# A two-layer vision tower on one core: tables shifted by products, column sums on VectorE, zeros in pieces, and a new order of the work

## The chip, the cores and the metric

One Trainium2 chip, one of its cores. The time is the device time of one execution in microseconds. Five engines run their own lists of instructions: PE (TensorE), DVE (VectorE), ACT (ScalarE), POOL (GpSimd) and SP, which only issues DMAs. Sixteen DMA engines serve all of them.

## What is computed

```python
h = tok(x, cls_token, cls_pos, ln1, W, bias, ln2)       # (32, 37, 256)
h = concatenate([cls_tok, h], axis=1)                   # (32, 38, 256)
h = h + attn0(layernorm(h))      # 16 heads, causal; weights rounded to -2..2 times their mean |w|
h = h + tanh(layernorm(h) @ W1 @ W2 @ W3 + b)
h = h + attn1(layernorm(h))      # 16 heads, with biases and a mask of heads
h = h + moe(layernorm(h))        # 16 experts of 256-1024-256, top 1, capacity ceil(1216 / 16)

def tok(img, ...):
    x = patches(img)                                    # 6 x 6 patches of 16 x 16 x 3 = 768
    x = layernorm(x) * ln1_g + ln1_b
    x = layernorm(x @ W + bias) * ln2_g + ln2_b
    return concatenate([cls_token + cls_pos, x + sincos_positions], axis=1)
```

Inputs, weights and result are fp32. 32 images of 38 tokens make 1216 rows, held as ten tiles of 128 rows (the last two have 116 and 76). As 38 doesn't divide 128, each tile starts at another phase of the image.

## The kernel before

**Token stage.** The image comes twice: by feature (`in_xf`, the left operand of the product, tile `xT`) and by token (`in_xt`, for the statistics), in five groups of tiles each, `XGROUPS` (L62). The first layernorm is folded into the weights: `tokWg` = `g1` * `tokW` minus a row of column sums. The column sums `cs` (L851 to L858) are six PE products of `gs` with the six blocks of `tokW`; DVE makes `tokWg` from them in six operations (L1259). The bias sums `bs` (L863) are six further products with `be1`. A token tile (`tok`, L897) is six products. DVE then scales it (L1300), takes its statistics (L1245, L1246), and in `tokn` normalises it (L1313) and adds the table of positions at the tile's phase (L1314). POOL forms the inverse roots (L768, L776).

**Tables.** POOL adds up one table `added` (L759). SP copies it with 16 DMAs into `attn1` at the phases of tiles 1 to 8 (`tables`, L521; L672 to L675). The real content of `attn1`, layer 1's weights, is loaded once DVE has the statistics of tile 8 (`a1`, L690 to L692). DVE's `wo` (L1289 to L1292) and PE's `bo` (L888) need it.

**Loads at the start.** SP and ACT issue them in a fixed order (L663 to L680, L1099 to L1109). SP's last four, two groups of `in_xf`, `in_ffn0` and all of `k_empty`, which presets the experts' buffer `expert_in` in HBM, stand behind the table copies. ACT sums the magnitudes of `attn0` (`asum`, L1126). DVE quantises it in `qs`, in six operations over long pieces (L1278 to L1282). PE folds the three matrices of the tanh block in `fB` and `fW` (L881).

**Attention.** Images go in pairs, 16 per layer. Per pair: POOL masks the keys by head (`km`, L791), PE makes the scores (`s`, L945, L950), DVE takes off their maxima (L1321, L1324), ACT the exponentials (L1164), PE transposes them (`pt`, L958) and multiplies with V (`pv`, L969), DVE divides (L1330, L1331), PE transposes again (`ot`, L975). V comes from L932; nine small DMAs per three images spread it over partitions (SP, L708), and POOL masks it (`vb`, L801). Q and K are made for 256 tokens at a time (`qk`, L921), the output projection per tile (`proj`, L983).

**Routing and experts.** Per tile: gate product (`log`, L990), DVE adds the bias, finds the largest value and its index and makes a one-hot row (L1352 to L1358), ACT sums the exponentials (L1182), PE counts (`cnt`, L998 to L1001), DVE makes the slot (L1363 to L1374), POOL scatters the token's row (`scat`, L824). Then twelve passes of expert work (L1024, L1035, L1057) with weights that SP streams in, and an indirect store per pass (L832). Ahead of them PE runs 58 records of filler (L1063).

**Order.** Each engine's order is fixed before the launch by `plan()`. It takes costs (`COST`), handover times (`HANDOVER`), arrival times of loads (`ARRIVES`, `XARRIVES`), and what each step needs (`needs()`). At each step it gives an engine the task with the least start time times `EAGER` plus due time (`wanted()`, from `GOAL`). Three PSUM buffers `G` go round among PE's steps in the order of `tasks`. An engine never leaves this order: where its next step has to wait, all behind it wait.

## Time and profile before

| | us |
|---|---|
| timed runs, median (lowest to highest of 3) | 361.92 (360.45 to 362.28) |
| the profiled execution | 361.07 |
| its span | 359.3 |
| PE busy | 325.1 |
| DVE busy | 195.7 |
| POOL busy | 168.6 |
| ACT busy | 167.7 |

The span runs from the first instruction to the last. Busy time leaves out register and DMA-issuing instructions; matmuls are pipelined and their ends are modelled, so a stretch in which PE is shown busy need not be at its peak. A group's row gives its busy time, the mean of one instruction, and the idle time of the engine before it with what ended that. A matmul in fp32 makes two records.

### The profile page before, as it was taken

Reading aid. Unit: us, or ns where it says so; the run is one execution under the profiler, and the core shown is the slowest. Engines: PE = TensorE matmul, PEld = TensorE weight load, DVE = VectorE, ACT = ScalarE, POOL = GpSimd, SP = SyncE. Lnnn points to the kernel's source line nnn. Section 1 sums busy time; section 2 is a strip of 40 time slices with the busy share of each in tenths; the row PEclk is TensorE's granted clock in tenths of the full one; section 3 lists DMA queues with packets and bytes.
Section 4 is the critical chain, followed back from the end, with each engine's and each line's share of the span. In section 5 each row is a group of like instructions: output and inputs, shape, how many; then the busy total and the mean of one; then the engine's idle time right before and its main releaser. Section 6 shows DMA issues by size and latency. Waiting matters only on the chain.

```text
span 359.3 us, 8864 instructions
## 1 busy us (share of the span) xinstructions
PE 325.1 (90%) x3230; PEld 233.9 (65%) x3230; DVE 195.7 (54%) x521; ACT 167.7 (47%) x473; POOL 168.6 (47%) x289
## 2 busy tenths in 40 slices
PE   2980999998599999999999999859999999999993
PEld 2860887776487888888888887549356455454361
DVE  1386286575557684587668798781152252351350
ACT  1580684743345666656665555540253243341350
POOL 0255189947346796669786776752002102012012
PEclk9996799999899999999999999977999999999998
DMA  7999901113521375144315242413999999993400
GB/s 232 410 361 374 392 10 55 56 53 115 203 97 58 110 223 179 51 154 158 119 48 167 87 138 80 171 37 113 397 374 409 350 359 359 315 376 103 158 12 10
DMA packets 40834, 67.11 MB, mean 187 GB/s; under 512 B 4941, under 2 KB 31888, under 8 KB 39960
## 3 DMA queue, kind: packets, MB, share of 16 engines
q1 hardware_dynamic: 36696, 57.29, 46.3%
q10 hardware_dynamic: 2448, 7.03, 5.3%
q0 software_dynamic: 1648, 2.24, 1.8%
q8 instruction: 26, 0.43, 0.5%
q14 instruction: 16, 0.13, 0.1%
HBM read 54.14 MB, written 8.48 MB: 174 GB/s over the span
## 4 chain that ended last, share of the span: by engine, by line
PE 57%; SPq 25%; DMA 8%; issue 3%; DVE 3%; POOL 2%; ACT 1%; POOLq 0%; DVEq 0%; ACTq 0%
SPq L708 21%; PE bank L1057 12%; PE bank L1024 12%; PE bank L921 5%; PE bank L1035 3%; DMA early<-in_ffn 3%; PE bank L897 3%; PE bank L932 3%; SPq L675 3%; DMA mid<-in_table 3%; PE bank L950 3%; PE bank L969 3%; PE bank L1063 2%; PE bank L983 2%; PE bank L958 2%
## 5 line engine op out<-in xcount | busy, mean ns | idle before, releaser
L832 POOL DMA_INDIRECT out<-mid,idx x12 | 11.7, 979 | 98.0 <-DVE mid L1411 98.0
L791 POOL TENSOR_TENSOR mid<-mid,tab 128x608 f32<-128x608 f32 x32 | 38.6, 1213 | 11.3 <-PE bank L950 10.6
L1057 PE MATMUL bank<-early,mid 128*64 128x256 f32 (+1 forms) x448 | 43.7, 381 | 0.0
L1207 ACT ACTIVATE mid<-bank,cols 128x64 f32<-128x64 f32 (+1 forms) x128 | 25.9, 333 | 25.1 <-PE bank L1035 25.1
L1024 PE MATMUL bank<-early,mid 128*64 128x512 f32 (+1 forms) x192 | 36.2, 596 | 0.7 <-ACT mid L1190 0.7
L1057 PEld LDWEIGHTS bank<-early,mid 128*64 128x64 f32 (+1 forms) x448 | 25.2, 123 | 15.8 <-issue 2.9
L921 PE MATMUL bank<-xnT,attn 128*128 128x256 f32 (+1 forms) x160 | 34.9, 371 | 0.0
L1164 ACT ACTIVATE mid<-mid 102x608 f32<-102x608 f32 x32 | 22.8, 713 | 20.9 <-DVE mid L1324 20.8
L1321 DVE TENSOR_REDUCE mx<-bank 102x16 f32<-102x608 f32 x32 | 25.0, 780 | 12.8 <-PE bank L950 12.5
L921 PEld LDWEIGHTS bank<-xnT,attn 128*128 128x128 f32 x160 | 29.1, 190 | 3.9 <-issue 0.8
L776 POOL TENSOR_TENSOR rs<-rs,mhalf 128x1 f32<-128x1 f32 (+2 forms) x50 | 29.0, 580 | 4.2
L897 PE MATMUL bank<-early 128*128 128x256 f32 (+2 forms) x120 | 27.4, 384 | 0.0
L1324 DVE TENSOR_TENSOR mid<-bank,mx 102x608 f32<-102x608 f32 x32 | 25.3, 792 | 1.1
L775 POOL TENSOR_SCALAR rs<-mv 128x1 f32<-128x1 f32 (+2 forms) x50 | 11.3, 227 | 29.5 <-DVE mv L1246 27.2
L897 PEld LDWEIGHTS bank<-early 128*128 128x128 f32 (+2 forms) x120 | 22.3, 188 | 3.9 <-ACT vt L1161 0.3
L932 PE MATMUL bank<-attn,xnT 128*114 128x256 f32 (+1 forms) x88 | 24.0, 397 | 0.0
L969 PEld LDWEIGHTS bank<-mid 120*38 120x38 f32 x768 | 19.7, 114 | 5.9 <-issue 3.0
L950 PE MATMUL bank<-mid 64*64 64x152 f32 (+1 forms) x512 | 23.2, 296 | 0.0
L958 PE MATMUL bank<-tab,mid 102*120 102x102 f32 x192 | 22.8, 255 | 0.0
L969 PE MATMUL bank<-mid 120*38 120x51 f32 (+1 forms) x768 | 22.8, 207 | 0.0
L1024 PEld LDWEIGHTS bank<-early,mid 128*64 128x64 f32 (+1 forms) x192 | 10.1, 123 | 19.3 <-issue 18.1
L1138 ACT ACTIVATE xn_gain<-tokens,nb,rs 128x256 f32<-128x256 f32 (+2 forms) x30 | 18.1, 602 | 9.1 <-POOL nb L783 8.6
(143 smaller groups left out, 661.5 us busy)
## 6 DMA issues: line engine op xcount, KB each, us to landing
early<-in_w SPq DMA_DIRECT2D x52, 512.0 KB, 6.7
v3a<-vt SPq DMA_DIRECT2D x102, 40.0 KB
early<-vt SPq DMA_DIRECT2D x90, 40.0 KB
expert_in<-k_empty SPq DMA_DIRECT2D x1, 3084.0 KB, 21.8
early<-in_xt ACTq DMA_DIRECT2D x2, 1152.0 KB, 20.6
early<-in_xf SPq DMA_DIRECT2D x2, 1152.0 KB, 12.0
xnT<-in_w SPq DMA_DIRECT2D x4, 512.0 KB, 7.7
tokens<-in_w SPq DMA_DIRECT2D x4, 512.0 KB
```

Of the source, the lines that this page charges most:

```text
L708: sp.dma_start(v3(first + a, 1)[j * KROW:(j + 1) * KROW, 0, :], vt[a * SEQ:a * SEQ + KROW, (m - 1) % 2, :]).then_inc(v_spread[(m - 1) % 2] ...
L776: ins = eng.tensor_tensor(rs[0:r, at, :], rs[0:r, at, :], bc(mhalf[0:r, :], 1, 1), ALU.pow)
L791: eng.tensor_tensor(km[:, n % 2], bc(kT[:, :, n * PCOLS:(n + 1) * PCOLS], 2, 4), bc(bc(quarterm[:, :], 2, PCOLS), 1, KC), ALU.mult).then_i ...
L897: mm_ = mm(ps[0:rows(n), 0:DIM], xT[:, n, j, 0:rows(n)], tokWg[:, j, :], start=j == 0, stop=j == PC - 1)
L921: ins = mm(ps[:, oc * width:(oc + 1) * width], w[:, kc, j * DIM + oc * 128:j * DIM + oc * 128 + 128], xnT[:, kc, gcols(n)], start=kc == 0, ...
L932: ins = mm(ps[0:vrows(n), 0:DIM], xnT[:, kc, vcols(n)], w[:, kc, 2 * DIM:3 * DIM], start=kc == 0, stop=kc == KC - 1)
L950: ins = mm(Sp[r0:r1, r, 4 * f * SEQ:4 * (f + 1) * SEQ], qT[half, f, q], km[half, n % 2, f, :, key], start=l == 1, stop=True, skip_group_ch ...
L958: ins = tr(PTp[0:KROWS, j, 0:PROWS], P[0:PROWS, n % 2, HSTART[j]:HSTART[j] + 3, :], ident[0:PROWS, 0:PROWS])
L969: ins = mm(Op[BROW * a:BROW * a + SEQ, h0 * VW:h1 * VW], PTs[0:KROWS, n % 2, j, a * SEQ:(a + 1) * SEQ], Vb[0:KROWS, (m - 1) % 3, a, h0:h1, ...
L1024: ins = mm(Hp[m % 2][a * width:(a + 1) * width, half, :], xeT[:, e, kc, at:at + width], w1s[e % W1_SLOTS][:, kc, half * 512:(half + 1) * 512],
L1057: ins = mm(Yp[m % 2][a * width:(a + 1) * width, 0:DIM], hT[:, m % 2, c, a * width:(a + 1) * width], w2s[e % W2_SLOTS][:, c, :], start=c == ...
L1207: ins = eng.activation(hT[:, m % 2, c, a * width:(a + 1) * width], Tp[0][:, c * 128 + a * width:c * 128 + (a + 1) * width], ACT.Relu, bias ...
```

## The change

Loads: `XGROUPS` has six groups. SP's table copies are gone, but for tile 8's two. `in_ffn0` goes to the place of `tokW` (tile `OT_`), so it waits for `tokWg` and `bs`. `a1` waits for nothing. `k_empty` is a sixth of its size and is written six times, as steps `z` in SP's order; its last column is 1. Tables: a matrix of shifted ones `k_turn` times `added` on PE (`tb`), into PSUM. Column sums: DVE weighs the blocks (`cw`), one product with ones adds them up over the partitions. Ten products of ones run first on PE. Quantisation: steps `qz`, V's weights first. Routing: the gate's bias by a product with one row, a copy on ACT, the one-hot row by comparing integers, no reciprocal per tile; the reciprocals move to the expert stage. The planner's numbers and due times are new.

```diff
-XGROUPS = [(0, 1), (1, 2), (2, 4), (4, 7), (7, 10)]
+XGROUPS = [(0, 1), (1, 2), (2, 4), (4, 6), (6, 8), (8, 10)]
+PIECES = 6
...
-PAIR, TILE, LAYER, EAGER = 6.69, 10.59, 113.2, 837.24
+PAIR, TILE, LAYER, EAGER = 6.69, 9.27, 112.7, 1000
...
-        "sp": {"v": 5.6, "a1": 3.0, "w": 2.2, "b2": 3.4}}
+        "sp": {"v": 5.6, "a1": 0.8, "z": 1.4, "w": 1.4, "b2": 3.4}}
...
-XARRIVES = [9.6, 11.5, 20.2, 28.7, 34.0]
+XARRIVES = [9.2, 11.5, 16.5, 22.5, 27.0, 31.5]
...
-        step("pool", "scat", 0, t, ("dve", "cnt", 0, t))
-    step("sp", "a1", 0, 0, ("dve", "lns", 0, TILES - 2))
+        step("pool", "scat", 0, t, ("act", "exp", 0, t), ("dve", "cnt", 0, t), ("sp", "z", 0, PIECES - 1))
+    step("sp", "a1", 0, 0)
...
-        if (e, kind) == ("dve", "tokn") and n:
-            at = max(at, 23.0)
...
+        tables = [added[:, :]] + [bank[n // 4][:, n % 4 * DIM:(n % 4 + 1) * DIM] for n in range(TILES - 3)] + [fv[:, 1, :], added[:, :]]
...
+        def weigh(queue, eng, by):
+
+            for j in range(PC):
+                if j in (0, PC // 2):
+                    queue.wait_ge(l_tokw[2 * j // PC], 16)
+                if j == 0:
+                    ins = eng.tensor_scalar(fv[:, 0, :], tokW[:, j, :], by[:, j:j + 1], None, ALU.mult)
+                else:
+                    queue.wait_ge(summed, j)
+                    ins = eng.scalar_tensor_tensor(out=fv[:, 0, :], in0=tokW[:, j, :], scalar=by[:, j:j + 1], in1=fv[:, 0, :], op0=ALU.mult, op1=ALU.add)
+                ins.then_inc(summed, 1)
...
             half_tokw(sp, 0)
             by_feature(0)
+            sp.dma_start(table, i["in_table"]).then_inc(l_table, 16)
             sp.dma_start(liveB[:, 0:DIM], i["in_live"][0, 0:DIM].partition_broadcast(128)).then_inc(l_bias, 16)
             by_feature(1)
-            sp.dma_start(table, i["in_table"]).then_inc(l_table, 16)
+            by_feature(2)
             half_attn0(sp, 0)
-            by_feature(2)
+            by_feature(3)
+            sp.wait_ge(tables_ready, 1)
+            for half in range(2):
+                at = (PHASES[TILES - 2] + 64 * half) % SEQ
+                sp.dma_start(tables[TILES - 2][64 * half:64 * half + 64, :], added[at:at + 64, :]).then_inc(phased, 16)
+            for j in range(4, len(XGROUPS)):
+                by_feature(j)
             sp.dma_start(maskb[:, :], k["k_mask"]).then_inc(l_mask, 16)
-            sp.wait_ge(tables_ready, 1)
-            for t in range(1, TILES - 1):
-                for half in range(2):
-                    at = (PHASES[t] + 64 * half) % SEQ
-                    sp.dma_start(tables[t][64 * half:64 * half + 64, :], added[at:at + 64, :]).then_inc(phased[t > 3], 16)
-            by_feature(3)
-            sp.dma_start(temp_[:, 0:3 * KC * DIM], i["in_ffn0"]).then_inc(l_ffn0, 16)
-            by_feature(4)
-
-            sp.dma_start(xbuf.rearrange("(p r) n -> p (r n)", p=128), k["k_empty"]).then_inc(l_zero, 16)
+            sp.wait_ge(tokw_ready, PC)
+            emptied(sp, uses[("bs", 0, 0)])
+            sp.dma_start(OT_[:, 0:3 * KC * DIM], i["in_ffn0"]).then_inc(l_ffn0, 16)
...
+                if kind == "z":
+                    at = XBUF // PIECES * n
+                    sp.dma_start(xbuf[at:at + XBUF // PIECES, :].rearrange("(p r) n -> p (r n)", p=128), k["k_empty"]).then_inc(l_zero, 16)
+                    continue
                 if kind == "a1":
-                    sp.wait_ge(mv_ready, stats_of[0].index(("lns", 0, TILES - 2)) + 1)
...
-                    pool.wait_ge(l_zero, 16)
+                    pool.wait_ge(se_ready, n + 1)
+                    pool.wait_ge(l_zero, 16 * PIECES)
...
+            pe.wait_ge(consts, 1)
+            for n in range(10):
+                mm(Sp[:, n % 2, 0:128], ones[:, :], ones[:, :], start=True, stop=True)
...
-                    for j in range(PC):
-                        ins = mm(ps[:, 0:DIM], gs[:, j:j + 1].to_broadcast([128, 128]), tokW[:, j, :], start=j == 0, stop=j == PC - 1)
-                    ins.then_inc(full, 1)
+                    mm(ps[:, 0:DIM], ones[:, :], fv[:, 0, :], start=True, stop=True).then_inc(full, 1)
...
+                elif kind == "tb":
+
+                    if n == 0:
+                        pe.wait_ge(l_turn, 16)
+                        pe.wait_ge(tables_ready, 1)
+                    for t in range(1 + 4 * n, min(5 + 4 * n, TILES - 2)):
+                        ins = mm(tables[t], shift[:, PHASES[t]:PHASES[t] + TROWS], added[0:SEQ, :], start=True, stop=True)
+                    ins.then_inc(turned, 1)
...
+                    if kind == "log":
+                        if m == 1:
+                            pe.wait_ge(l_live, 16)
+                        ins = mm(ps[0:rows(n), 0:EXP], ones[0:1, 0:rows(n)], bgB[0:1, :], start=False, stop=True)
...
                 elif kind == "log":
+                    act.wait_ge(g_full[b], g + 1)
...
+                    eng.copy(lg[0:rows(n), n % 2, :], G[b][0:rows(n), 0:EXP]).then_inc(g_free[b], 1)
+                elif kind == "exp":
...
-                    for w, inv in ((qkvT, 2), (projT, 3)):
-                        ins = eng.tensor_scalar(w, w, qs[:, inv:inv + 1], MAGIC, ALU.mult, ALU.add)
-                    link(ins)
-                    link(eng.tensor_scalar(attn0[:, :], attn0[:, :], MAGIC, -2.0, ALU.subtract, ALU.max))
-                    for w, c in ((qkvT[:, :, 0:DIM], 4), (qkvT[:, :, DIM:], 0), (projT, 1)):
-                        ins = eng.tensor_scalar(w, w, 2.0, qs[:, c:c + 1], ALU.min, ALU.mult)
-                    ins.then_inc(quant_ready, 1)
+                elif kind == "qz":
+
+                    w, inv, c = ((qkvT[:, :, 2 * DIM:], 2, 0), (qkvT[:, :, 0:DIM], 2, 4), (qkvT[:, :, DIM:2 * DIM], 2, 0), (projT, 3, 1))[n]
+                    link(eng.tensor_scalar(w, w, qs[:, inv:inv + 1], MAGIC, ALU.mult, ALU.add))
+                    link(eng.tensor_scalar(w, w, MAGIC, -2.0, ALU.subtract, ALU.max))
+                    eng.tensor_scalar(w, w, 2.0, qs[:, c:c + 1], ALU.min, ALU.mult).then_inc(quant_ready, 1)
...
-                    eng.tensor_tensor(lg[0:r, q, :], G[b][0:r, 0:EXP], bgB[0:r, :], ALU.add).then_inc(g_free[b], 1)
...
-                    link(eng.tensor_copy(idf[0:r, n:n + 1], ti[0:r, q, 0:1]))
-                    eng.tensor_scalar(oh[0:r, n, :], iota[0:r, :], idf[0:r, n:n + 1], None, ALU.is_equal).then_inc(oh_ready, 1)
+                    eng.tensor_tensor(oh[0:r, n, :], iotau[0:r, :], ti[0:r, q, 0:1].to_broadcast([r, EXP]), ALU.is_equal).then_inc(oh_ready, 1)
...
-                    eng.reciprocal(tokens[0:r, n, 2 * DIM + 1:ROW], se[0:r, n:n + 1])
```

In the planner's `needs()` the first scores also wait for `tokn` 4 and the first transposes for `tokn` 7 (`tables_used`), the first `ot` copy for `fW`, and `in_ffn0` no longer shares a place with the spread V.

## Rows read from the trace of the kernel before

**Rows 1.** the page, its head and part 1

```profile
span 359.3 us, 8864 instructions
...
PE 325.1 (90%) x3230; PEld 233.9 (65%) x3230; DVE 195.7 (54%) x521; ACT 167.7 (47%) x473; POOL 168.6 (47%) x289
```

**Rows 2.** stretches: length, busy PE, PEld, DVE, ACT, POOL, granted clock, DMA share, GB/s

```profile
0.00:25.40 25.40, 18.72 (x74) 15.72 (x74) 10.20 (x27) 12.55 (x26) 8.20 (x25) 1.00 0.92 335
25.40:35.30 9.90, 0.02 (x1) 0.00 (x0) 6.93 (x18) 1.54 (x5) 5.08 (x12) 0.70 1.04 362
35.30:39.90 4.60, 4.58 (x12) 3.74 (x13) 0.00 (x0) 0.77 (x2) 0.00 (x0) 0.54 1.17 478
...
80.00:97.00 17.00, 11.84 (x137) 8.65 (x140) 8.54 (x20) 6.17 (x14) 9.63 (x15) 0.92 0.49 168
97.00:220.00 123.00, 123.00 (x1582) 101.04 (x1574) 88.38 (x225) 73.83 (x184) 86.90 (x134) 1.00 0.37 120
220.00:242.80 22.80, 16.93 (x170) 12.28 (x165) 18.91 (x94) 11.02 (x37) 15.43 (x30) 0.88 0.28 95
...
252.60:354.10 101.50, 100.63 (x886) 50.64 (x886) 34.97 (x76) 34.88 (x147) 10.77 (x11) 1.00 0.79 281
2.00:44.00 42.00, 27.43 (x105) 23.07 (x106) 18.08 (x46) 18.83 (x42) 13.38 (x31) 0.88 1.02 376
```

**Rows 3.** the timeline, first hole and what stands around it

```profile
12.92 10.17 SPq L675 DMA_DIRECT2D attn<-added  x16
...
19.99 5.43 PE L897 MATMUL bank<-early 128*128 128x256 f32 x24
...
35.31 3.78 PE L881 MATMUL bank<-early 128*128 128x256 f32 x8 [9.90 <-DMA early<-in_ffn]
...
49.79 1.03 PE L932 MATMUL bank<-attn,xnT 128*114 128x256 f32 x4
```

**Rows 4.** DMA view, 0 to 45 us; the last number of an issue is us to landing

```profile
DMA packets 4526, 15.89 MB, mean 353 GB/s; under 512 B 619, under 2 KB 2283, under 8 KB 3947
...
expert_in<-k_empty SPq DMA_DIRECT2D x1, 3084.0 KB, 21.8
```

**Rows 5.** the timeline, second hole

```profile
91.96 0.69 DVE L1289 TENSOR_TENSOR hmh<-tab,liveB 128x16 f32<-128x16 f32 x1 [4.36 <-DMA attn<-in_attn]
...
93.56 1.54 PE L888 MATMUL bank<-attn,cols 128*128 128x256 f32 x4 [3.64 <-DVE attn L1292]
```

**Rows 6.** the timeline at the start: start us, us, engine line op

```profile
6.68 5.46 PE L857 MATMUL bank<-mid,gs 128*128 128x256 f32 x12 [6.68 <-DMA mid<-in_tokw]
...
11.93 2.90 PE L863 MATMUL bank<-mid,cols 128*128 128x256 f32 x12
...
12.18 2.44 DVE L1259 SCALAR_TENSOR_TENSOR early<-mid,cols,bank 128x256 f32<-128x256 f32 x6 [10.23 <-PE bank L857]
```

**Rows 7.** the timeline, DVE and GpSimd side by side

```profile
57.49 2.54 POOL L791 TENSOR_TENSOR mid<-mid,tab 128x608 f32<-128x608 f32 x2
...
57.57 1.40 DVE L1313 SCALAR_TENSOR_TENSOR tokens<-tokens,mv,xn_gain 128x256 f32<-128x256 f32 x1 [3.27 <-POOL rs L781]
```

**Rows 8.** groups of lines, shapes apart

```profile
L1282 DVE TENSOR_SCALAR attn<-attn,qs 128x512 f32<-128x512 f32 x2 | 1.0, 483 | 0.0
```

**Rows 9.** groups of DVE, 231 to 246 us: busy us, mean ns, idle before

```profile
L1352 DVE TENSOR_TENSOR lg<-bank,liveB 128x16 f32<-128x16 f32 (+2 forms) x5 | 0.8, 169 | 0.1
...
L1357 DVE CAST idf<-ti 128x1 f32<-128x1 uint32 (+2 forms) x5 | 0.8, 152 | 0.2
L1363 DVE RECIPROCAL tokens<-se 128x1 f32<-128x1 f32 (+2 forms) x5 | 0.8, 152 | 0.7 <-ACT ex L1182 0.7
```

**Rows 10.** SP's queue in the timeline, and the scatter's own row

```profile
51.31 13.67 SPq L708 DMA_DIRECT2D v3a<-vt  x18
...
215.02 9.01 SPq L708 DMA_DIRECT2D v3a<-vt  x12
...
L824 POOL DMA_INDIRECT expert_in<-tokens,sloti x10: 994/1087/1287, 197.5 to 244.9; - x10
```

147 lines of the change are left out of this document (94 added, 53 removed), and 7 rows, old and new, of the table GOAL.

## The prediction

> **What bounds the kernel now.** I read the page first. The profiled execution has a span of 359.3 us and took 361.07 us, 1.8 us around the span; the three timed runs have their median at 361.92 us, so it stands 0.85 us below that median. TensorE is busy for 325.1 us, nearly twice any other engine [rows 1]. Then I cut the span by TensorE's busy time [rows 2]. From 97 to 220 us it is busy for 123.00 of 123 us, from 252.6 to 354.1 us for 100.63 of 101.5 us. What can be won lies in the rest: the start (18.72 busy of 25.4 us), a hole (0.02 of 9.9 us), a slow piece behind it at a granted clock of 0.54, a second hole (11.84 of 17 us, clock 0.92) and the end of the routing (16.93 of 22.8 us).
>
> A busy TensorE may still be waiting inside its pipeline. LDWEIGHTS, which has no modelled end, is busy for 101.04 of 123 us in the full stretch and 15.72 of 25.4 us at the start. The Trainium skill ("Trainium Kernel Development and Optimization", Performance Expectations) calls MFU and LDWEIGHTS share the good measures and matmul busy time a bad one. By it TensorE would have 18% slack from 97 to 220 us. I keep the row of idle time: nothing is named that TensorE stood still for there, and that it might have slack is the first rival.
>
> The first hole: SP issues 16 table copies one after another from 12.92 to 23.1 us, and only behind them the last two groups of `in_xf`, `in_ffn0` and all of `k_empty` (3084 KB, 21.8 us to landing) [rows 3, 4]. All 16 DMA engines are full from 2 to 44 us at 376 GB/s [rows 2]. TensorE's own order puts `fB` ahead of token tile 4, so it stands until `in_ffn0` lands and starts L881 at 35.31 us at half clock: 3.78 us for 8 records, where full clock needs half, 1.9 us [rows 3]. The second hole: `attn1` holds the shifted tables until the token tiles are done, so its weights are asked for late; DVE stands 4.36 us for them at 91.96, and TensorE's `bo` comes at 93.56 after 3.64 us idle [rows 5].
>
> **The change, part by part.**
>
> *Start.* Before, TensorE makes the column sums in 5.46 us and then the bias sums, the same number of products of the same size, in 2.90 us [rows 6]; the granted clock reads 1.00 over both [rows 2], but the first run at half the second's pace, as if at 1.2 and not 2.4 GHz. The first token tile starts behind both, near 14.8 us. After, ten products of ones run first, then the bias sums. They cost between 2.90 us (warm, L863) and 5.46 us (like L857), so they end between 8.3 and 10.9 us from a start at 5.4. Beside them DVE weighs the six blocks: six operations of the size of L1259, 2.44 us plus five waits on itself of 0.05 to 0.1 us, say 3.0 us. The last half of `tokW` is there at 6.68 us, where L857 stops waiting for it; the first three blocks fit before that, so the sum is ready at 8.2. One product (0.45 us, a twelfth of L897's 5.43 us for two tiles of six [rows 3]) and the first piece of `tokWg` (0.48 us) follow. Token tile 0 can start between 9.3 and 11.9 us.
>
> Those six operations have two SBUF inputs. One such operation, L1313, took 1.40 us as GpSimd began L791 beside it [rows 7]. At 1.40 us each the weighing would end at 13.5 us. GpSimd has one addition to do in this stretch, so I take the short time. The Trainium skill ("GPSIMD Engine Reference", Key points) speaks against this edit: it has GpSimd share its SBUF interfaces with VectorE operations that have two SBUF inputs. The row at 57.57 agrees.
>
> *Tables.* The seven products of 256 columns add 7 x 0.44 = 3.1 us to TensorE. They remove 14 of 16 issues from SP (8.9 us) and 896 KB from the DMA engines. Tables 1 to 7 stay in PSUM, in the banks of the scores; the first scores wait for `tokn` 4 and the first transposes of P for `tokn` 7. TensorE has the rest of the token tiles, V and Q/K to do until then, about 30 us, so I put this wait at nothing.
>
> *Loads.* Before, 15.89 MB move until about 44 us [rows 4]. Without `k_empty`, 14 tables, `in_ffn0` and the mask, some 10.85 MB stand ahead of the last group (both copies of the image 7.86, `tokW` 0.79, `attn0` 1.05, small tables and rows 1.15): at 376 GB/s from 2 us on, it lands at about 31 us. TensorE then needs tiles 2 and 3 at about 17, 4 and 5 at 23, the last two at 32 or later: arrival and need match. `in_ffn0` follows at about 33, `attn1` at 37 to 39. Ahead of `in_ffn0` SP now waits for `tokWg` and `bs`; `attn1`, the zeros and the V spreads queue behind it, but both are there by 14 us and none of those is wanted before 37, so this costs nothing. `a1`, moved up past every V step, takes its one issue out of SP's full stretch.
>
> *Sum up to the first V product* (49.79 us before [rows 3]; cs, bs, qs, eight token tiles, `fB`, one lnt are done by then). After, from tile 0 at 9.3 to 11.9: eight tiles 8 x 2.72 = 21.7, tables 3.1, fB 1.9, qs and lnt 0.7: 36.7 to 39.3 us. I take 37.5, a gain of **12.3 us**. All 16 tables copied by DMA, the hole, the half-speed `fB` and the cold column sums are in it. The bound from below is DVE: it has 3.0 + 2.6 + 8 tiles x 1.1 + 5 `tokn` x 1.0 + the quantisation in the same 31 us, near 27, and any wait in its order shows; I put the gain no lower than 6. Above: 14.
>
> *Quantisation.* Six long operations become twelve of 0.483 us, 5.8 us against 4.2, on DVE [rows 8]. V and Q/K can begin after the first and third part. The cover is TensorE's token tiles; without it 1.6 us would show. I take 0.
>
> *Second hole.* Of 17 us, 5.16 are idle, and clock 0.92 costs 1.4 more; about 1 us of it stands before `attn1` is in play. With `attn1` there by 39 I take a gain of **5.5 us**, bounds 0 (something else is late next: the key masks on GpSimd) and 6.5.
>
> *Routing.* Per tile DVE loses a bias addition (169 ns), a cast (152 ns) and a reciprocal (152 ns) [rows 9], with gaps some 0.55 us, four tiles' worth on the chain behind 233 us: 2.2 us. ScalarE's copy and a further product with one row stand in front of DVE instead: no row has them alone, between 0.1 and 0.6 us per tile; on the chain of the last tile, 0.5, and on a full TensorE before it 10 x 0.1 = 1 us. Net gain **0.7 us**, bounds -1 and 2. Twelve reciprocals in the expert stage: DVE is busy 35 of 101.5 us there; nothing.
>
> *SP.* Six issues of zeros of about 0.5 us replace one of 1.4 at an idle time. At the end SP spreads V without a pause: 12 issues in 9.01 us [rows 10], 0.75 us each, 4.5 us per pair. The extra 3 us are at nothing if they fall into its pauses, 3 us if not.
>
> Sum: 12.3 + 5.5 + 0.7 = 18.5 us. Span 340.8, execution 361.07 - 18.5 = 342.6; in terms of the median 343.4. I say **343.0 us**.
>
> **The rivals.**
> 1. *The attention stretch is not TensorE's.* DVE, or GpSimd with its masks, sets the start of the scores and the holes come back elsewhere. For it: LDWEIGHTS at 82%, and DVE at 88.38 of 123 us. Against: no named TensorE idle from 97 to 220. Half the 17.8 us of both holes would be lost: **352 us**.
> 2. *SP's V spreads become the bound.* 192 of them are 144 us, its other issues 12; before, it had 172 us for them, from 51.31 to 224 us [rows 10]. If the first V product comes at 37.5 it has some 166 us. For it: SP has no pause over the last 24 issues. Against: 10 us of room. It would give back 3 to 8 us: **349 us**.
> 3. *Slower.* GpSimd waits in order at the first scatter for all six pieces of zeros. The order places a piece as if a V step took SP 5.6 us, but nine issues are 6.75 us. If the last piece comes behind its place, GpSimd stops masking keys, and TensorE runs dry a pair later. First scatter before: 197.5 us [rows 10]. Each us that the last landing passes its time is a us lost; it decides once it is over 18.5 us late, and SP can be late by 22 x 1.15 = 25 us: **365 us**. Against: V steps wait for their data anyway, which takes the lateness out.
> 4. *The change does not do what it says*: the last group lands no earlier, since the queues share engines by another key; only the second hole, the start's 3 us and the routing are won: **352 us**.
>
> **How the numbers follow.** My forecast 0.70, rival 1 0.12, rival 2 0.08, rival 3 0.04, rival 4 0.03, and 0.03 for a hole that I don't see. All but rival 3 and a part of the last are faster by over 0.5% (1.8 us, about what a measurement of this kernel tells from no change): faster 0.93, same 0.02, slower 0.05. The bounds of the terms alone give 335 to 354; the likeliest case spans 337 to 348. The range 335 to 352 takes in the first two rivals.
>
> **What would show it.** Right: the first token tile near 10 us; no TensorE idle over 2 us between 10 and 45 us with the clock at 1; the first V product at 36 to 40 us; `bo` without a wait; DMA full until about 38 and not 44 us; the last scatter near 227 us and the expert stage as long as before, 101 to 102 us. Wrong: DVE without a gap from 5 to 45 us while TensorE waits for it; GpSimd idle in front of L824 by DMA; SP unbroken through layer 1 with GpSimd's L801 waiting for it; an expert stage of another length.

## The result and the profile after

The changed kernel takes **352.92 us** (median of 4 runs, 351.87 to 353.66) where the one before takes 361.35 us in the same session. The ratio is 0.9749, with a 95% interval of 0.9703 to 0.9796. The forecast was 343.0 us, with a range of 335 to 352: faster was right, 18.5 us were forecast and 8.4 came, and the time lies outside the range. Some executions show a lower granted clock and a longer time; the medians given here take in all executions, the ratios leave those out.

The page of the kernel after, head and part 1, as in [rows 1]:

```profile
span 351.8 us, 8970 instructions
...
PE 331.7 (94%) x3274; PEld 238.4 (68%) x3274; DVE 195.4 (56%) x516; ACT 169.8 (48%) x483; POOL 166.9 (47%) x289
```

The span is 7.5 us shorter, and TensorE is busy for 6.6 us more. So its idle time fell by 14.1 us, and about half of that was filled again with its own work. The rest says where.

Windows of the kernel after, with the columns of [rows 2] (the last two are held against 97 to 220 and 252.6 to 354.1 us of before: the first of them ends 7.5 us earlier, the last has the same length at another place):

```profile
0.00:25.40 25.40, 23.16 (x89) 18.88 (x90) 11.32 (x30) 9.60 (x20) 6.12 (x22) 0.87 0.94 340
25.40:35.30 9.90, 9.20 (x44) 7.82 (x44) 8.84 (x26) 9.10 (x22) 7.06 (x18) 1.00 1.01 411
35.30:39.90 4.60, 4.60 (x23) 4.06 (x22) 4.32 (x12) 3.92 (x11) 2.30 (x7) 1.00 0.11 42
...
80.00:97.00 17.00, 17.00 (x260) 14.04 (x258) 10.86 (x22) 9.09 (x22) 10.40 (x14) 1.00 0.25 81
97.00:212.50 115.50, 113.02 (x1406) 91.64 (x1398) 80.71 (x199) 68.81 (x172) 84.35 (x131) 1.00 0.43 141
...
245.10:346.60 101.50, 100.61 (x886) 50.62 (x886) 36.90 (x88) 34.76 (x147) 10.74 (x11) 1.00 0.79 281
```

Both holes are closed, and the expert stage is as long as before. But the clock reads 0.87 over the first 25 us, and from 97 us on 2.5 us of idle time have appeared where there was none.

The timeline of TensorE at the start, to be held against [rows 3, 6]:

```profile
1.15 4.17 PE L883 MATMUL bank<-ones 128*128 128x128 f32 x20 [1.15 <-POOL ones L783]
5.16 3.13 PE L901 MATMUL bank<-mid,cols 128*128 128x256 f32 x12
8.72 0.67 PE L893 MATMUL bank<-fv,ones 128*128 128x256 f32 x2 [0.43 <-DVE fv L643]
9.94 4.83 PE L909 MATMUL bank<-added,shift 38*128 38x256 f32 x14 [0.55 <-DMA shift<-k_turn]
14.71 12.41 PE L943 MATMUL bank<-early 128*128 128x256 f32 x48
27.81 0.35 PE L916 MATMUL bank<-asum,ones 128*128 128x2 f32 x2 [0.70 <-issue]
28.03 10.61 PE L943 MATMUL bank<-early 128*128 128x256 f32 x48
38.47 1.89 PE L927 MATMUL bank<-mid 128*128 128x256 f32 x8
42.41 0.41 PE L952 MATMUL bank<-tab,xn_gain 128*128 128x128 f32 x2 [2.05 <-issue]
42.83 1.99 PE L927 MATMUL bank<-mid 128*128 128x256 f32 x8
44.66 1.03 PE L978 MATMUL bank<-attn,xnT 128*114 128x256 f32 x4
45.53 1.03 PE L934 MATMUL bank<-attn,cols 128*128 128x256 f32 x4
```

The first V product (L978) comes at 44.66 us: 5.1 us earlier than before, not 12.3. The first scores gain even less. They come at 60.09, where before they came at 60.47, because token tile 9, `bo`, a third V product and one more turned tile now stand ahead of them. `bo` (L934) has no wait any more.

ScalarE at the same time, by its timeline and by its waits (waited for: us in total, times, longest) up to 45 us:

```profile
41.73 0.59 ACT L1195 ACTIVATE xn_gain<-tokens,nb,rs 128x256 f32<-128x256 f32 x1
...
42.86 0.37 ACT L1198 COPY xnT<-bank 128x256 f32<-128x256 f32 x1
```

```profile
ACT early L1177 <- DMA early<-in_xt: 8.3, 5, 2.7
```

ScalarE's first normalisation stands in its order behind all ten statistics. It starts at 41.73 us, and TensorE's 2.05 us in front of L952 are that wait. Before, ScalarE waited 2.6 us for `in_xt` and stood 12.1 us for `fB`: it had time in hand. Now it has none. It is also fed later. These are the issues of `in_xt` of before and after (the first and last start are in us; below each, the time to landing):

```profile
L1098 ACTq DMA_DIRECT2D early<-in_xt x5: 453/534/785, 1.7 to 6.3; - x5
DMA to landing us min/median/max: 8.5/15.3/22.2
L1153 ACTq DMA_DIRECT2D early<-in_xt x6: 358/542/857, 2.2 to 7.6; - x6
DMA to landing us min/median/max: 9.7/19.8/29.9
```

In both it is the last one that takes longest. So the last `in_xt` group landed at 28.5 us before and lands at 37.5 now, while the last `in_xf` group landed at 38.1 us before (issued at 24.3, 13.8 us) and lands at 30.3 now (10.2, 20.1 us). The change brought one copy of the image forward and pushed the other back.

The DMA view up to 60 us (KB each, median us from issue to landing) shows what moves beside them:

```profile
early<-in_xf SPq DMA_DIRECT2D x4, 768.0 KB, 16.5
early<-in_xt ACTq DMA_DIRECT2D x4, 768.0 KB, 23.6
attn<-in_attn SPq DMA_DIRECT2D x1, 1024.0 KB, 25.0
...
mid<-in_ffn SPq DMA_DIRECT2D x1, 768.0 KB, 22.7
```

`in_ffn0` was issued at 12.50 us, and `in_attn1` at 12.87; it landed at 37.9. ScalarE's last image group let its statistics start at 37.47. The Trainium skill ("Trainium Kernel Development and Optimization", Key Constraints) has the DMAs of SP and ACT run on the same 16 engines and interleave. These rows agree: the forecast had 10.85 MB ahead of the last group, but the 1.84 MB of `in_ffn0` and `in_attn1`, issued behind the image groups, moved beside them, and 12.90 MB were through by 38 us.

### The profile page after: what moved, and what is told of

Its sections match the earlier page's. It is cut to its first block, busy times and chain, and to the rows that moved or that the text cites. A ratio compares the mean times of both kernels' runs of the same rounds, so it can differ in the third digit from the quotient of the medians.

```text
span 351.8 us, 8970 instructions
## 1 busy us (share of the span) xinstructions
PE 331.7 (94%) x3274; PEld 238.4 (68%) x3274; DVE 195.4 (56%) x516; ACT 169.8 (48%) x483; POOL 166.9 (47%) x289
## 4 chain that ended last, share of the span: by engine, by line
PE 69%; SPq 15%; issue 6%; POOL 3%; DMA 3%; ACT 1%; DVE 1%; ACTq 0%; POOLq 0%
SPq L741 13%; PE bank L1112 12%; PE bank L1079 12%; PE bank L943 6%; PE bank L967 5%; PE bank L1034 4%; PE bank L1007 4%; PE bank L1090 3%; PE bank L1018 3%; PE bank L997 3%; PE bank L978 3%; PE bank L1118 3%; DMA shift<-k_turn 2%; PE bank L1041 2%; PE bank L952 2%
## 5 line engine op out<-in xcount | busy, mean ns | idle before, releaser
L1195 ACT ACTIVATE xn_gain<-tokens,nb,rs 128x256 f32<-128x256 f32 (+2 forms) x30 | 18.0, 600 | 22.9 <-POOL nb L816 22.8
L943 PE MATMUL bank<-early 128*128 128x256 f32 (+2 forms) x120 | 28.4, 398 | 0.0
L943 PEld LDWEIGHTS bank<-early 128*128 128x128 f32 (+2 forms) x120 | 23.3, 196 | 4.8 <-issue 0.7
L978 PE MATMUL bank<-attn,xnT 128*114 128x256 f32 (+1 forms) x88 | 23.1, 385 | 1.3 <-ACT xnT L1198 1.3
L834 POOL TENSOR_TENSOR mid<-v3a,tab 120x512 f32<-120x512 f32 x17 | 17.9, 1057 | 12.6 <-DMA v3a<-vt 5.2
L834 POOL TENSOR_TENSOR mid<-early,tab 120x512 f32<-120x512 f32 x15 | 16.3, 1084 | 15.4 <-issue 7.9
L997 PE MATMUL bank<-mid 64*38 64x152 f32 (+1 forms) x512 | 22.9, 293 | 0.3 <-issue 0.3
L1079 PEld LDWEIGHTS bank<-early,mid 128*64 128x64 f32 (+1 forms) x192 | 10.1, 123 | 19.3 <-issue 18.1
## 6 DMA issues: line engine op xcount, KB each, us to landing
early<-in_xf SPq DMA_DIRECT2D x4, 768.0 KB, 16.5
early<-in_xt ACTq DMA_DIRECT2D x4, 768.0 KB, 23.6
```

What stands on the lines that cost most here:

```text
L834: eng.tensor_tensor(Vb[0:KROWS, (m - 1) % 3, :, :, 0:HD], v3(2 * (m - 1), 2).rearrange("p a (h d) -> p a h d", h=HEADS), bc(bc(blockm[:, : ...
L943: mm_ = mm(ps[0:rows(n), 0:DIM], xT[:, n, j, 0:rows(n)], tokWg[:, j, :], start=j == 0, stop=j == PC - 1)
L978: ins = mm(ps[0:vrows(n), 0:DIM], xnT[:, kc, vcols(n)], w[:, kc, 2 * DIM:3 * DIM], start=kc == 0, stop=kc == KC - 1)
L997: ins = mm(Sp[r0:r1, r, 4 * f * SEQ:4 * (f + 1) * SEQ], qT[half, f, q], km[half, n % 2, f, :, key], start=l == 1, stop=True, skip_group_ch ...
L1079: ins = mm(Hp[m % 2][a * width:(a + 1) * width, half, :], xeT[:, e, kc, at:at + width], w1s[e % W1_SLOTS][:, kc, half * 512:(half + 1) * 512],
```

## The experiments

Eighteen kernels ran. The table gives, from each profiled execution, the start of the first V product, of the first scores, of the last PV product and of the last count (us), and beside them the median and the ratio to the kernel before. Single executions of one kernel differ by 1 to 1.5 us at the first scores (compare `after` with e17, and e12 with e19, which are the same kernel). The kernels ran in five groups on five chips, each beside the kernel before: e1 to e4, e5 to e8, e10 to e13, e14 to e16, e17 to e19. Across groups only ratios can be compared, and even they move: the kernel of e12 came to 0.9652 and, as e19 on another chip, to 0.9745.

| kernel | V | scores | last PV | last count | median | ratio, 95% |
|---|---|---|---|---|---|---|
| before | 49.79 | 60.47 | 227.79 | 242.72 | 361.35 | |
| after | 44.66 | 60.09 | 221.38 | 235.24 | 352.92 | 0.9749, 0.9703 to 0.9796 |
| e1_hold | 43.95 | 59.37 | 220.07 | 233.91 | 352.29 | 0.9719, 0.967 to 0.9768 |
| e2_tables_two | 45.86 | 60.60 | 224.63 | 238.49 | 353.39 | 0.9755, 0.9712 to 0.9799 |
| e3_no_warm | 45.42 | 61.23 | 221.65 | 235.54 | 352.74 | 0.9734, 0.968 to 0.9788 |
| e4_hold_tables | 44.28 | 59.02 | 218.72 | 232.57 | 352.62 | 0.9772, 0.9722 to 0.9821 |
| e5_qs_late | 44.69 | 61.35 | 220.45 | 234.30 | 352.29 | 0.9722, 0.9685 to 0.9758 |
| e6_qs_late_hold | 43.71 | 61.22 | 220.56 | 234.40 | 352.50 | 0.9728, 0.9689 to 0.9767 |
| e7_bias_dve | 44.47 | 59.75 | 219.96 | 234.22 | 351.85 | 0.9702, 0.9656 to 0.9748 |
| e8_three | 43.71 | 61.22 | 219.05 | 233.30 | 351.47 | 0.9703, 0.9657 to 0.9749 |
| e10_half_stats_hold | 42.67 | 59.95 | 219.60 | 233.35 | 350.72 | 0.9678, 0.9633 to 0.9722 |
| e11_bo_late | 43.67 | 57.61 | 229.97 | 243.72 | 360.92 | 0.9960, 0.9934 to 0.9987 |
| e12_z_first | 44.36 | 59.12 | 219.14 | 232.88 | 349.84 | 0.9652, 0.9613 to 0.9691 |
| e13_replanned | 46.49 | 54.87 | 219.25 | 232.59 | 349.36 | 0.9620, 0.9572 to 0.9669 |
| e14_replan_z | 43.65 | 52.03 | 217.54 | 231.37 | 350.45 | 0.9705, 0.965 to 0.976 |
| e15_replan_z_bias | 44.47 | 52.70 | 226.37 | 239.31 | 357.14 | 0.9894, 0.986 to 0.9929 |
| e16_z_bias | 44.13 | 59.68 | 215.61 | 230.01 | 349.69 | 0.9720, 0.9674 to 0.9767 |
| e17_unchanged | 45.82 | 61.07 | 220.62 | 234.51 | 352.14 | 0.9746, 0.9713 to 0.978 |
| e18_twelve | 45.79 | 60.55 | 225.64 | 239.53 | 357.50 | 0.9881, 0.9838 to 0.9923 |
| e19_z_first_again | 45.26 | 60.58 | 219.78 | 233.64 | 351.77 | 0.9745, 0.9704 to 0.9786 |

### One limit of the start at a time

**e1_hold.** The two transfers wait for the last image groups.

```diff
+            sp.wait_ge(l_xt[5], 16)
+            sp.wait_ge(l_xf[5], 16)
             sp.dma_start(OT_[:, 0:3 * KC * DIM], i["in_ffn0"]).then_inc(l_ffn0, 16)
```

> SyncE issues ffn0 and attn1 (1.84 MB) only once the last image groups of both orientations have landed. Theory L (the loads: these two share the DMA engines ahead of the last groups, and that alone took the gain of the start): 1.84 MB at 376 GB/s is 4.9 us, so ScalarE's wait for its last group ends at about 33 in place of 37.5, the first V product goes from 44.7 to 40.5 to 41.5, and the time falls by 3 to 4 us, to about 349.5. Theory T (TensorE has no free time left in the start: 10 warm-up products, 7 table products and 6.4 us at the 1.2 GHz level fill what the column sums and the waits gave back): only the 2.05 us of idle time before the first turned tile can go, the first V product comes at 42.6 or later, and the time falls by 0.5 to 1.5 us, to 351.5 to 352.5.

**e2_tables_two.** Five of the seven table products are left out.

```diff
-                    for t in range(1 + 4 * n, min(5 + 4 * n, TILES - 2)):
+                    for t in (1 + 4 * n,):
...
-        tables = [added[:, :]] + [bank[n // 4][:, n % 4 * DIM:(n % 4 + 1) * DIM] for n in range(TILES - 3)] + [fv[:, 1, :], added[:, :]]
+        tables = [added[:, :]] + [bank[n // 4][:, 0:DIM] for n in range(TILES - 3)] + [fv[:, 1, :], added[:, :]]
```

> Five of the seven shifted tables aren't made (their tiles take another tile's table: part of the computation is left out), the two others and every order stay. Theory L: no change (353), since the last group's landing doesn't move. Theory T: some 3.4 of 4.83 us go from TensorE ahead of the first image product, which starts at about 11.3 in place of 14.7; but in the orders as written the first turned tile still waits for ScalarE's last statistics (41.8), so most of it becomes idle time there and the time falls by 0 to 1 us.

**e3_no_warm.** Without the loop of ten products at L883.

> The ten warm-up products are left out. If they are what puts TensorE at full clock (granted clock 1.00 from 1 to 11 us), bs (3.13 us) and the sums then run at the 1.2 GHz level, as the first products of the kernel before did (5.46 us for 12): about 2 us later at the first image product, and the time is 353 to 355. If the warm-up is what the half-clock stretch from 11.7 to 18.2 is the price of, that stretch goes or moves ahead to 5 to 10 us, and the time is 351.5 to 353.

**e4_hold_tables.** e1 and e2 in one.

> The hold of ffn0 and attn1 and the five missing table products together. Theory L: the same as the hold alone. Theory T: both limits of the start are lifted at once, so the gains are more than the sum of the two alone: first image product at 11.3, last group at 33, first V product at 39 to 40 in place of 44.7, and the time falls by 3.5 to 5 us, to about 348.5.

None can be told from the changed kernel. The hold did end ScalarE's wait for the last group (it landed at 33.4 us, not 37.5), but its normalisation started at 40.50 in place of 41.73: it had been fed late by the earlier groups (its tile 4 started at 27.75, at 28.32 without the hold), and six tiles at 2.13 us each lie behind that. The warm-up made no difference that shows either: without it the bias sums took 5.45 us in place of 3.13, and tile 0 still started at 13.94, not later than 14.71. Theory L wanted the first V product at 40.5 to 41.5 us in e1, and it came at 43.95, 0.7 us earlier than in the changed kernel. Theory T's "more than the sum" did not come either: e4 was no faster. Its timeline, TensorE in front of `qs`, shows where its 4 us went:

```profile
27.39 0.56 PE L918 MATMUL bank<-asum,ones 128*128 128x2 f32 x2 [6.07 <-issue]
```

TensorE finished its first four token tiles at 21.3 us (e2 has the same wait, 6.34 us), and then stood 6 us for `qs`, the product over ScalarE's weight sums. So the next two moved `qs`, with a planned order edited by hand (each entry is put right behind the second one):

```diff
+MOVES = [("pe", ("qs", 0, 0), ("tok", 0, 5)), ("dve", ("qs", 0, 0), ("tok", 0, 5)), ("dve", ("qz", 0, 0), ("qs", 0, 0)),
+         ("dve", ("qz", 0, 1), ("tok", 0, 6)), ("dve", ("qz", 0, 2), ("tok", 0, 7)), ("dve", ("qz", 0, 3), ("tokn", 0, 5))]
```

**e5_qs_late** is this alone, **e6_qs_late_hold** has the hold too.

> Only two orders change: TensorE's qs moves from ahead of token tile 4 to behind token tile 5, and VectorE's qs and the four parts of the quantisation move behind token tiles 5, 5, 6, 7 and tokn 5. Theory Q (the one that the first four runs suggest: in each of them TensorE stood or arrived at qs at 27.0 to 27.7 us, since ScalarE's weight sums stand behind xs 3 and the loads, so nothing gained ahead of 27 us counts): TensorE goes on with tile 4 as soon as its group has landed, at 25 to 26, at most 2 us earlier than 28.0. Alone, with the loads as they are, the first turned tile still waits for ScalarE's last statistics at 41.8: time 352 to 353, no change that can be told. Theory L (loads only): the same. A time over 354 would say that the quantisation then stands in front of a token tile on VectorE.

> The same two orders, with ffn0 and attn1 held until the last image groups have landed. Theory Q: the hold alone left TensorE idle for 3.88 us ahead of qs and then 6 us at half clock; both go. Token tile 4 starts at 23.5 to 25, no half-clock stretch follows at 30 to 36, ScalarE's last statistics end at about 37 to 38, and the first V product comes at 39.5 to 41 in place of 43.95: time 348.5 to 350. Theory S (the start doesn't count at all, something later takes up whatever it gains): the first V product moves but the last count and the time don't: 352 to 353.

Theory Q fell. The wait ahead of `qs` is gone, and it stands elsewhere. Timeline of e6:

```profile
31.90 0.28 PE L927 MATMUL bank<-asum,ones 128*128 128x2 f32 x2
32.04 5.43 PE L954 MATMUL bank<-early 128*128 128x256 f32 x24
38.59 1.99 PE L938 MATMUL bank<-mid 128*128 128x256 f32 x8 [1.13 <-DMA mid<-in_ffn]
41.46 0.41 PE L963 MATMUL bank<-tab,xn_gain 128*128 128x128 f32 x2 [0.87 <-issue]
```

The first turned tile (L963) comes at 41.46, as in e1 (41.28). The next kernel therefore keeps all of e6 and halves ScalarE's statistics (the mean is left out):

```diff
-                    link(eng.activation(here, here, ACT.Identity, accum_out=xsum[:, n, :]))
-                    link(eng.activation(xmean[:, n, :], xsum[:, n, :], ACT.Copy, scale=-1.0 / (PC * 128)))
-                    eng.activation(here, here, ACT.Square, bias=xmean[:, n, :], accum_out=xvar[:, n, :]).then_inc(xs_ready, 1)
+                    eng.activation(here, here, ACT.Square, accum_out=xvar[:, n, :]).then_inc(xs_ready, 1)
```

> ScalarE's statistics of an image tile are cut from three operations to one (the mean is left out, so each tile's variance is that about zero), 2.13 us to 1.1 us; the hold of ffn0 and attn1 and the late qs of the run before are kept. Theory C (ScalarE is what the start now waits for: in all runs so far its ten statistics and the weight sums end at 40.5 to 41.8 us and the first normalised tile, in its order behind all ten, follows at 41.3 to 42.5, whatever was lifted on TensorE or the loads): ScalarE is through at 35.5 to 37, the first V product comes at 39.5 to 41, and the first scores at 57.5 to 59 in place of 61.2; time 348.5 to 350.5. Theory T (TensorE has no time to spare there anyway): the first V product moves by 1 us or less and the first scores stay at 60 to 61: 352 to 352.5.

ScalarE had ten us less work, and its first normalisation came 5.3 us earlier than in e6 (35.43 against 40.78). The first V product came 1.0 us earlier (42.67 against 43.71), the first scores 1.3 (59.95). TensorE's timeline says why it was no more:

```profile
13.90 17.88 PE L954 MATMUL bank<-early 128*128 128x256 f32 x72
...
38.17 1.99 PE L938 MATMUL bank<-mid 128*128 128x256 f32 x8 [0.99 <-DMA mid<-in_ffn]
40.00 0.38 PE L963 MATMUL bank<-tab,xn_gain 128*128 128x128 f32 x2
```

It turns the first tile as soon as its own work ahead of it is done, with 0.99 us of waiting for `in_ffn0`. So the direction of theory C holds, and the 1 us is what theory T said. Then tiles 8 and 9 and `bo` stand ahead of the first scores, and those take their 6.4 us. **At least four things end close together in the start: `qs`, `in_ffn0`, ScalarE's statistics and TensorE's own work. Taking one away uncovers the next: hold, late `qs` and half the statistics together bring 2.0 us at the first V product.**

### The second hole by itself

**e11_bo_late** puts `attn1`, `wo` and `bo` back where they stood.

```diff
+MOVES = [("sp", ("a1", 0, 0), ("v", 0, 4)), ("dve", ("wo", 0, 0), ("lns", 1, 0)), ("dve", ("bo", 0, 0), ("s", 0, 6)),
+         ("pe", ("bo", 0, 0), ("lnt", 0, 7))]
```

> attn1 is issued behind the fifth V spread, and wo and bo stand where they stood before the change (VectorE behind the statistics of layer step 1 of tile 0, TensorE ahead of the seventh V product); nothing else changes. This is the second hole alone. If its removal is worth what the prediction gave it (5.5 us), VectorE waits again for in_attn near 90 us, the granted clock falls behind it, and the time is 356 to 359. If the hole was bound by something else and the gain came from other edits, no wait on in_attn shows and the time is 352 to 353.5; part of it would be back if the wait is there but under 2 us.

It is 8 us slower than the changed kernel (its ratio, 0.9960, against 0.9620 to 0.9678 of the other three on its chip), and nearly as slow as the kernel before. Timeline of e11:

```profile
88.85 0.18 DVE L1366 TENSOR_TENSOR hmh<-tab,liveB 128x16 f32<-128x16 f32 x1 [6.39 <-DMA attn<-in_attn]
89.94 2.08 PE L943 MATMUL bank<-attn,cols 128*128 128x256 f32 x4 [8.40 <-DVE attn L1369]
```

This hole is deeper than the one of before (8.40 us in front of `bo` against 3.64 [rows 5]). `attn1` was asked for at 83.7 us, 2.6 us earlier than before, but TensorE came to `bo` 8.4 us earlier (81.5 against 89.9). So 8 us is more than the change won there. The windows measure both, 61 to 100 us (columns of [rows 2]), for e11, before and after:

```profile
61.00:100.00 39.00, 26.93 (x365) 21.26 (x363) 15.81 (x31) 15.49 (x35) 19.37 (x31) 0.87 0.33 109
```

```profile
61.00:100.00 39.00, 33.76 (x376) 26.16 (x369) 23.38 (x46) 17.20 (x36) 24.66 (x41) 0.96 0.31 103
100.00:220.00 120.00, 120.00 (x1554) 98.50 (x1552) 86.80 (x223) 73.30 (x183) 85.69 (x133) 1.00 0.38 122
```

```profile
61.00:100.00 39.00, 37.59 (x509) 30.57 (x509) 22.51 (x41) 22.28 (x49) 27.65 (x42) 1.00 0.29 91
100.00:220.00 120.00, 117.27 (x1480) 95.11 (x1478) 84.93 (x217) 71.57 (x183) 85.23 (x133) 1.00 0.44 145
```

Idle time there is 12.07, 5.24 and 1.41 us. Against before, the change won 3.83 us of it, and the clock of 0.96 over 39 us was 1.6 more: 5.4 us. By the same count e11 loses 10.66 us of idle time and 5.1 of clock (0.87), 15.7 us, against the changed kernel, and 8.5 us of them are left at the last count. By that share the hole of before was worth 2.9 us. So it was worth 3 to 5.4 us.

### The gate's bias

**e7_bias_dve** lets VectorE add it again; **e8_three** joins hold, late `qs` and this.

```diff
-                        ins = mm(ps[0:rows(n), 0:EXP], ones[0:1, 0:rows(n)], bgB[0:1, :], start=False, stop=True)
...
-                    eng.copy(lg[0:rows(n), n % 2, :], G[b][0:rows(n), 0:EXP]).then_inc(g_free[b], 1)
...
+                    eng.tensor_tensor(lg[0:r, q, :], G[b][0:r, 0:EXP], bgB[0:r, :], ALU.add).then_inc(g_free[b], 1)
```

> The gate's bias goes back to VectorE, as in the kernel before: the product with one row and ScalarE's copy of the logits leave, VectorE adds the bias on its way out of PSUM; all else as in the changed kernel. If the product costs what its rows show (0.39 us for two records, ten times, of which about 0.33 lies behind the other records, on a TensorE without idle time), the last count comes 2.5 to 3.5 us earlier, at about 232.5 in place of 235.2, and the time is 349.5 to 350.5. If it costs what the prediction gave it (0.1 us per tile), the time is 352 to 352.5. If the VectorE steps that the change took out mattered more than the product, it is slower than 353.

> The hold, the two orders and the bias on VectorE together. Theories Q and the product's price add up: 3 to 4 us plus 2.5 to 3.5 us, a time of 346 to 347.5. If the start doesn't count (theory S), only the bias shows: 349.5 to 350.5.

The group of the product in the changed kernel, 97 to 220 us (busy us, mean ns of one record; two records per tile):

```profile
L1045 PE MATMUL bank<-liveB,ones 1*128 1x16 f32 x10 | 1.9, 268 | 0.0
```

A product with one row and 16 columns is not cheap: the two records of a tile last 0.39 us together, and 0.33 us of that lies behind the records ahead of them. Yet only 1.1 us came back by the median (intervals overlap). At the last PV product e7 is 1.4 us earlier, at the last count 1.0: from one to the other e7 takes 14.26 us, the changed kernel 13.86, so 0.4 us of what TensorE saves goes back on the chain of the last tiles.

### SyncE's queue

**e12_z_first** issues the zeros ahead of the first V spread, behind a wait for the last `in_xt` group; **e18_twelve** sends each piece as two halves of the same bytes in its old place; **e17_unchanged**, the changed kernel, and **e19_z_first_again**, the kernel of e12, ran beside e18.

```diff
+MOVES = [("sp", ("z", 0, 0), ("a1", 0, 0))] + [("sp", ("z", 0, x), ("z", 0, x - 1)) for x in range(1, 6)]
...
                 if kind == "z":
+                    if n == 0:
+                        sp.wait_ge(l_xt[5], 16)
```

> All six pieces of zeros are issued ahead of the first V spread, once the last image group has landed; 6 x 0.57 = 3.4 us of issuing leave SyncE's unbroken stretches. Rival 2 of the prediction (SyncE's V spreads set the pace): 1.5 to 3.5 us faster, 349.5 to 351.5, with the last V spread earlier by as much. If TensorE sets the pace from 60 us on (busy for 98% of 80 to 220 us): no change, 352.5 to 353.5.

> Each piece of zeros goes out as two halves of the same bytes together, at the same six places: 12 issues in place of 6 on SyncE among the V spreads, about 3.4 us more of issuing. If SyncE's issuing sets the pace there (rival 2), 2 to 3.5 us slower than the unchanged kernel, and the last V spread 2 to 3.5 us later. If TensorE does, within 1 us of it.

> The changed kernel as it is, on the same chip as the next two, so that the zeros' places are compared side by side (0, 6 and 12 issues among the V spreads). Both theories: 352 to 353.5.

> The zeros ahead of the V spreads once more, beside the other two. If rival 2 holds, 2 to 3 us faster than the unchanged kernel, as before. If the 3.1 us of that run were chance and chip, within 1 us of it.

The first run gave 3.1 us, the second beside the unchanged kernel 0.4. So no gain is shown for moving the zeros. Twelve issues cost 5.4 us against six. SyncE's timeline in e18, the first two halves:

```profile
54.25 1.22 SPq L725 DMA_DIRECT2D expert_in<-k_empty  x2
```

and TensorE's largest named wait in e18, 61 to 222 us:

```profile
PE bank L953 <- ACT xn_gain L1196: 3.1, 3, 1.7
```

Zero, six and twelve issues give 351.8, 352.1 and 357.5 us: a knee. The change put SyncE's queue right at its edge: the six more issues take 3.8 us of its time (7.1 against 3.3 us in all) and cost 5.4. The windows from 100 to 220 us of e17 and e18 hold most of it:

```profile
100.00:220.00 120.00, 118.80 (x1493) 97.02 (x1491) 87.17 (x224) 72.97 (x184) 87.75 (x135) 1.00 0.44 145
100.00:220.00 120.00, 115.60 (x1420) 93.74 (x1418) 83.59 (x205) 70.01 (x177) 85.75 (x131) 0.99 0.43 138
```

TensorE stands 3.2 us more, and behind waits of 1.02 and 0.61 us at 156 us its granted clock reads 0.95 from 140 to 160 us and 0.96 from 160 to 180, which is 1.8 us more. Together that is the 5.0 us by which e18's last PV product is later. Rival 2 is not shown to have taken the gain, but SyncE is the next thing late.

### New orders

**e13_replanned** gives the planner the arrivals of the trace, and due times chosen anew for them.

```diff
-XARRIVES = [9.2, 11.5, 16.5, 22.5, 27.0, 31.5]
+XARRIVES = [11.9, 16.3, 21.3, 28.3, 30.5, 37.5]
...
-           ... ("act", "asum"): 19.5 ... ("pe", "fB"): 34.0 ... ("pe", "tb"): 8.2
+           ... ("act", "asum"): 25.0 ... ("pe", "fB"): 35.5 ... ("pe", "tb"): 9.7
```

> The planner gets the arrivals that the trace shows (image groups at 11.9, 16.3, 21.3, 28.3, 30.5, 37.5 us in place of 9.2 to 31.5; attn0 for the weight sums at 25.0 and not 19.5; in_ffn0 at 35.5, k_turn at 9.7) and 0.9 us for a gate product with its bias, and its due times were chosen anew for these. In its orders ScalarE normalises and copies tiles 0 and 1 before the last statistics, the first scores stand ahead of the last token tile, and V 1 to 3 between scores. Theory C (the order was planned for loads that come 2.7 to 6 us later than assumed, and ScalarE's order makes all wait for the last of them): first scores at 54 to 56 in place of 60.1, and the time 349 to 350.5. Theory T: the start is TensorE's own work, so other orders only exchange it: 352 to 353.5.

> The new orders (planned with the arrivals of the trace) and the zeros ahead of the V spreads together. If the 3.5 us and the 3.1 us that the two gave alone have separate causes (ScalarE's order in the start; SyncE's unbroken issuing from 46 to 105 us), they add: 345.5 to 347. If both only move the same slack (TensorE's work from 60 us on is the bound either way, and single executions differ by 1 us in where the half-clock stretch falls), the two together are no faster than the better of them: 349 to 350.

> As the run before, with the gate's bias back on VectorE and the orders chosen once more for that. The product's rows give 10 x 0.33 us on TensorE, while the trace of the kernel with that edit alone ended only 1.0 us earlier at the last count (234.2 against 235.2). If TensorE's work is the bound from 60 us on, 2 to 3 us less than the run before: 343.5 to 345. If VectorE's addition gives it back on the last tile's chain, 0 to 1 us less.

> The changed kernel's own orders, with the zeros ahead of the V spreads and the bias on VectorE. Against 349.84 us for the zeros alone this is the bias's price once more: 348.5 to 349 if its trace told the whole (1 us), 346.5 to 347.5 if the product's rows do (3.3 us on a full TensorE), 349.8 or more if it costs nothing.

e13 has **the lowest ratio of all, 0.9620** (0.9572 to 0.9669), some 4.5 us better than e17 (0.9713 to 0.978). But e17 ran on another chip. e12, on e13's chip, lay below e17 in the same way, and its kernel did not repeat that; and e14, which has e13's orders, came to 0.9705. So a gain in time of these orders is not shown. What the traces show is the order's effect on the start, and there theory C holds in direction. In its timeline TensorE turns the first tile ahead of `qs`, and the scores start 5.2 us earlier:

```profile
26.09 0.41 PE L948 MATMUL bank<-tab,xn_gain 128*128 128x128 f32 x2 [2.38 <-issue]
28.16 0.56 PE L912 MATMUL bank<-asum,ones 128*128 128x2 f32 x2 [1.67 <-issue]
```

But the last PV product gained only 2.1 of those 5.2 us (1.4 against e17). What stands ahead of the scores in one order stands behind them in the other, and TensorE does all of it. e14 had its scores at 52.03 and its last PV product 3.1 us ahead of e17's; its ratio cannot be told from e17's. e15 let the planner believe in cheap SyncE issues (0.65 us in place of 1.4 for an expert load), and it placed more of the expert loads early: the DMA rate from 61 to 100 us is 186 GB/s, in e14 141. It is slower than e14 by 7 us, with 7.35 us of idle TensorE from 100 to 220 us. That it fell over the knee that e18 shows fits, but isn't tested. e16 has the earliest last count of all, 230.01, and a median of 349.69; its ratio (0.9720) can't be told from that of e7 (0.9702), so no gain of the zeros shows there either.

## Why the prediction was wrong

**The sign and both holes.** Right. Both holes closed. The second was forecast at 5.5 us and measured at 3 to 5.4.

**The start: this is the step that failed.** 12.3 us were forecast at the first V product; 5.1 came. The sum had TensorE's own work alone on the path (27.4 us from tile 0 on) and put the loads ("arrival and need match") and ScalarE at nothing. The runs show two paths of nearly the same length in its place.

ScalarE's path: the first group is there at 11.9 us. Ten tiles at 2.13 us and 2.3 for the sums make 23.6 us, that is 35.5. ScalarE stood again for groups that came at 16.3, 21.3, 28.3 and 37.5 us, 6.1 us in all (the order had been planned for 11.5, 16.5, 22.5 and 31.5). That gives 41.7 us for the first normalisation, whatever TensorE does. I had checked TensorE and VectorE as bounds of the start, and not ScalarE.

TensorE's path: from my 37.5 to the measured 44.66 us are 7.2 us, and the timeline holds them:
- Tile 0 starts at 14.71. The 37.5 us have it at 13.2 (10.1, and 3.1 for the tables). The seven table products took 4.83 us, not 3.1, partly at the 1.2 GHz level: 1.5 us late.
- Tiles 0 to 3 took 12.4 us from start to start, tiles 4 to 7 10.4, together 22.8 where I had 21.7: 1.1 us, the granted clock again.
- 0.7 us of standing ahead of `qs`.
- 2.05 us of standing ahead of the first turned tile, ScalarE's order.
- `fW`, 1.8 us net: it stands ahead of the first V product now and stood behind it before. I compared two moments with different work behind them. The line of before:

```profile
50.88 1.89 PE L881 MATMUL bank<-early 128*128 128x256 f32 x8
```

These are no separate causes. In e12 the tables (3.29 us) and the first four tiles ran at full clock, TensorE then stood 4.04 us for `qs`, and the first V product came at 44.36. In e10 ScalarE was through by 35.43, and TensorE's own work held the first V product at 42.67. The weighing by VectorE was priced rightly: its five operations with two inputs took 484 ns by their median, 829 at most.

**The range.** The bounds of the terms were added up wrongly. The start (6 to 14), the second hole (0 to 6.5) and the routing (-1 to 2) make 5 to 22.5 us, so, from the 361.92 us that I started from, 339 to 357 us and not 335 to 354. The measured 352.92 lies in that.

**What was given back later.** An account from single executions closes at the last count (7.5 us earlier) like this. First scores 0.4 us earlier, with 4.9 us of work moved ahead of them (tile 9 2.65, `bo` 1.0, a V product 0.95, a turned tile 0.3): 5.3 us. Second hole 5.4 us. Last PV to last count 1.1 us less. Against it 2.7 us of new idle time from 100 to 220 us and 1.6 us for five gate products there. 11.8 less 4.3 is 7.5. The new idle time I had not priced at all; in e17, the same kernel, it is 1.2 us.

**Routing.** Forecast 0.7 us won. Measured: 1.1 us less behind the last PV, 1.6 us of products ahead of it, so 0.5 us lost. The product was mis-sized: 0.33 us per tile, in place of 0.1. e7 fits: without it the last count is 1.0 us earlier.

**Quantisation.** Right at nothing: no wait on its parts shows, and e5 could place it 2.4 us later.

**SyncE.** Put at nothing, with 10 us of room. There was less: from 46.2 to 164.3 us it has no pause over 0.6 us, which I had named as a sign of rival 2 (for layer 1), GpSimd's masking of V (L834) waited 16.8 us in all for spreads where L801 had waited 9.3, and e18 finds the edge within 3.8 us. Taking the zeros out of that stretch (e12, e19) won 3.1 and 0.4 us, so no loss by them is shown.

**The rivals.** Rival 4 (the last group lands no earlier; 352 us, chance 0.03) is nearest to what happened: the last group of all landed at 38.1 us before and at 37.5 after. But the landing alone does not make it: e1 brought the last `in_xt` group to 33.4 us, and the first V product moved by 0.7. Its chance was far too low, with both queues on the same engines. Rival 1 said that TensorE might not set the stretch from 97 us on. From 100 to 220 us LDWEIGHTS is busy for 95.11 of 120 us. By the Trainium skill's measure ("Trainium Kernel Development and Optimization", Performance Expectations) that would be 21% slack, an estimate. Against slack speaks that scores 5 and 8 us earlier (e13, e14) brought 2.1 and 3.8 us at the last PV product, or 1.4 and 3.1 against e17: what was pulled ahead of that stretch was mostly pushed back into it. That is an argument and no test. Rival 3 fell: no scatter waited for zeros, and the first one came at 190.8 us.

**Not settled.** Why new idle time arises after 100 us isn't tested; it stood at 1.2 to 2.7 us in the two traces of the changed kernel, so part of it may be chance. Nor were tables by DMA from a second queue tried in place of the products; e2 says only that fewer products alone win nothing.
